# Two residual linear layers with LoRA on one core: where W0's transposition, the small stores and the second weight blocks stand

## The reference

```
x = x + (x W0^T + b0 + (x A0^T) B0)            # base_weight W0, A0, B0 per batch by adapter id
x = x + (x W1^T + b1 + 2 (x A1) B1)            # SCALING = 32/16 = 2
```

## Time and profile before

| | |
|---|---|
| median of 3 runs | 2171.0 us (2167.95 to 2177.97) |
| the profiled execution | 2161.93 us, its span 2160.2 us |
| PE busy | 2076.9 us, 96% of the span |
| DVE busy | 1535.8 us, 71% |
| ACT busy | 738.1 us, 34% |
| POOL busy | 689.3 us, 32% |
| mean DMA rate | 212 GB/s |
| weight matmuls | 3 x 2688 of 128 x 128 x 512 |

### The profile page before, as it was taken

How to read it: one execution, slowest core, us unless ns; L and a number is a source line. 1 busy time by engine, 2 the same in 40 slices (tenths; PEclk the granted TensorE clock), 3 DMA queues, 4 the chain that set the end, 5 groups by cost and what they waited for, 6 DMA issues and landing times.

```text
span 2160.2 us, 27571 instructions
## 1 busy us (share of the span) xinstructions
PE 2076.9 (96%) x9292; PEld 1712.8 (79%) x9292; DVE 1535.8 (71%) x2161; ACT 738.1 (34%) x1294; POOL 689.3 (32%) x498
## 2 busy tenths in 40 slices
PE   6599899999989999999999999999999999999999
PEld 5488687887878788888887888877888788888887
DVE  3367778867778876676876666875767876766875
ACT  5453232323323332333333333332333333333332
POOL 0023121544030445140544130544221445221353
PEclk9799999999999999999999999999999999999999
DMA  9974746798664699474799574789574689574676
GB/s 294 279 239 128 234 145 196 213 277 262 176 185 140 201 266 304 143 222 131 213 259 311 146 224 119 225 246 293 168 217 122 213 242 321 168 215 123 209 218 198
DMA packets 316681, 458.03 MB, mean 212 GB/s; under 512 B 27516, under 2 KB 125820, under 8 KB 316028
## 3 DMA queue, kind: packets, MB, share of 16 engines
q1 hardware_dynamic: 316284, 455.21, 69.9%
q10 hardware_dynamic: 256, 1.05, 0.3%
HBM read 381.70 MB, written 74.45 MB: 211 GB/s over the span
## 4 chain that ended last, share of the span: by engine, by line
PE 73%; DVE 9%; DMA 9%; issue 3%; SPq 2%; ACT 2%; POOL 1%; ACTq 0%; DVEq 0%; POOLq 0%
PE acc L1497 22%; PE acc L1499 21%; PE acc L1498 21%; DMA w_second<-wc_t 4%; DVE w_lo L1031 3%; DMA w_second<-v_t 2%; PE h_acc L1410 2%; PE h_acc L1414 2%; DVE c_out L1193 2%; DVE x_sum L1046 1%; DMA pb_t<-b1d_rows 1%; POOL w_raw L804 1%; DVE c_acc L1132 1%; DVE xop_lo L1056 1%; PE acc L1424 1%
## 5 line engine op out<-in xcount | busy, mean ns | idle before, releaser
L1497 PE MATMUL acc<-xop_hi,w_hi 128*128 128x512 f32 x2688 | 1055.6, 393 | 24.2 <-DVE w_lo L1031 19.1
L804 POOL TENSOR_TENSOR w_raw<-w_raw,w_second 128x512 f32<-128x512 f32 x464 | 652.3, 1407 | 1280.5 <-DMA w_second<-wc_t 862.9
L1498 PE MATMUL acc<-xop_hi,w_lo 128*128 128x512 f32 x2688 | 1048.9, 390 | 0.0
L1499 PE MATMUL acc<-xop_lo,w_hi 128*128 128x512 f32 x2688 | 1048.7, 390 | 0.0
L1031 DVE TENSOR_TENSOR w_lo<-w_raw,w_hi 128x512 fp32r<-128x512 f32 x672 | 568.3, 848 | 446.8 <-ACT w_hi L869 443.7
L869 ACT ACTIVATE w_hi<-w_raw 128x512 fp32r<-128x512 f32 x672 | 423.7, 631 | 1194.7 <-PE acc L1499 980.8
L1497 PEld LDWEIGHTS acc<-xop_hi,w_hi 128*128 128x128 f32 x2688 | 506.2, 188 | 142.1 <-DVE w_lo L1031 31.1
L1499 PEld LDWEIGHTS acc<-xop_lo,w_hi 128*128 128x128 f32 x2688 | 506.1, 188 | 106.4
L1498 PEld LDWEIGHTS acc<-xop_hi,w_lo 128*128 128x128 f32 x2688 | 506.4, 188 | 103.0
L1193 DVE TENSOR_TENSOR c_out<-acc,c_out 128x512 f32<-128x512 f32 x304 | 202.1, 682 | 7.9 <-PE acc L1424 6.2
L1046 DVE TENSOR_TENSOR x_sum<-x_in 128x512 f32<-128x512 f32 x240 | 207.5, 876 | 0.1
(11 more groups left out here) (117 smaller groups left out, 826.7 us busy)
## 6 DMA issues: line engine op xcount, KB each, us to landing
w_raw<-wc_t SPq DMA_DIRECT2D x448, 256.0 KB, 3.8
w_second<-wc_t SPq DMA_DIRECT2D x320, 256.0 KB, 5.0
w_raw<-v_t SPq DMA_DIRECT2D x208, 256.0 KB, 3.8
w_second<-v_t SPq DMA_DIRECT2D x144, 256.0 KB, 5.0
x_in<-x_t SPq DMA_DIRECT2D x128, 256.0 KB, 6.0
out_t<-c_out SPq DMA_DIRECT2D x128, 256.0 KB, 5.4
x_in<-w_t SPq DMA_DIRECT2D x64, 256.0 KB, 5.8
wc_t<-c_out SPq DMA_DIRECT2D x64, 256.0 KB, 5.5
```

The lines of the kernel that those rows point to most:

```text
L804: nc.gpsimd.tensor_tensor(w_raw[:, r, :], w_raw[:, r, :], w_second[:, n % RAW2, :], ALU.add if sign > 0 else ALU.subtract).then_inc(w_summ ...
L1497: nc.tensor.matmul(bank[:, :], wh, xh, start=(k == 0), stop=False)
L1498: nc.tensor.matmul(bank[:, :], wl, xh, start=False, stop=False)
L1499: mm = nc.tensor.matmul(bank[:, :], wh, xl, start=False, stop=end)
```

## The change

- **Transposition of W0.** Units: 4 instead of 8 (a quarter of W0). Parts: 24 instead of 16 (three quarters). Parts are numbered in a list `PARTS`, with the step of M5 at which each is transposed (four still ahead of it) and a list `PART_G_AT` with the step at which its share of G is made: up to two parts in a step, and two G's in M3. G now stands ahead of the step's own matmuls on PE. Four loaded parts are held instead of three.
- **Small stores.** q_rows, qd_rows and b1d_rows are stored at step 2 of M5 instead of in the preamble. b1's rows aren't stored from SBUF: eight DMAs from DRAM to DRAM in M1 bring them to `pb_t`. The loads of b1's rows, of the first parts and of W1's first block stand earlier in the preamble. The load of block (0, 0) of W1 moves to steps 0 and 1 of M3.
- **A1 + A1 W0.** `ag` takes 2 A1 W0 alone, copied by ACT; A1 is loaded again (`a1_row`) and added in passes 2 to 5.
- **U B0 and U b0 spread out.** `p_add` at steps 4, 9, 14, 19 instead of 4, 8, 12, 16; M2's `down` after steps 5 and 7, with the split for M4's at step 12; the second half of `scale_c` in M7 instead of M4; its `turn_c` in M6.
- **Second blocks by ACT's queue.** `load_second`: ACT issues the DMA of `w_second` for step g+5 right behind `w_hi` of step g+2.

The core of the diff:

```diff
+DOWN_AT, A_SPLIT_AT = (1, 3), 8
+DOWN_LATE, A_SPLIT_LATE = (5, 7), 12
...
-    UNITS = [(mg, dg) for dg in (2, 3) for mg in range(GROUPS)]
+    UNITS = [(mg, 2) for mg in range(GROUPS)]
...
-    E_AFTER, Q_AFTER = 3, 5
+    E_AFTER, Q_AFTER = 2, 3
...
-    NPART = 16
-    PIN, PRAW = 3, 4
+    FIRST = [(u // 4, u // 2 % 2 + 2 * (u % 2), at)
+             for u, at in enumerate((-1, -1, -1, -1, 0, 1, 2, 2, 5, 5, 6, 7, 8, 9, 10, 11))]
+    LAST = [(6 + i // 4, i % 4, at) for i, at in enumerate((3, 3, 4, 4, 12, 13, 14, 15))]
+    PARTS = sorted(FIRST + LAST, key=lambda p: p[2])
+    PIN, PRAW = 4, 4
+    PART_G_AT = [1, 1, 2, 2, 3, 3, 4, 4, 5, 5, 6, 6, 7, 7, 8, 9, 10, 11, 12, 13, 14, 15, 16, 17]
...
-        P_ADD_AT = (4, 8, 12, 16)
+        P_ADD_AT = (4, 9, 14, 19)
+        C_TURN_AT = ((M7, 2), (M6, 6))
...
@@ SP, load_w @@
-                for oh, dh in second:
...
-                    sp.dma_start(w_second[:, n % RAW2, :], w_t[oh * MH + m, :, col:col + SW]
-                                 ).then_inc(wb_loaded[n % RAW2], 16)
@@ SP, load_a @@
+                sp.dma_start(a1_row[:, :, :], lora_a1[bass.ds(adapter_of(1, b), 1), :, :]
+                             .rearrange("o p (k r) -> (o p) k r", r=RANK)).then_inc(a1_row_loaded, 16)
@@ SP, preamble @@
-                if t == 1:
                     for b in range(BATCH):
                         sp.dma_start(b1_rows[b * RANK:(b + 1) * RANK, :],
...
-                if t == 4:
+                if t == 1:
                     sp.wait_ge(a1_lo_ready, 1)
                     sp.wait_ge(t_filled, B_USE + 4)
+                    for n in range(PIN):
+                        load_part(n)
                     for k in range(KH):
                         load_x(0, 1, 1, k)
...
-                    sp.dma_start(q_t[:, :], q_rows[:, :]).then_inc(small_stored, 16)
-                    sp.dma_start(qd_t[:, :], qd_rows[:, :]).then_inc(small_stored, 16)
-                    for i, rows in enumerate((b1_rows[:, 0:DIM // 2], b1_rows[:, DIM // 2:], b1d_rows[:, :])):
-                        sp.dma_start(pb_t[i, :, RANK:R2, :], rows).then_inc(small_stored, 16)
@@ SP, loop over g @@
                 if g == 2:
+                    sp.dma_start(q_t[:, :], q_rows[:, :]).then_inc(small_stored, 16)
+                    sp.dma_start(qd_t[:, :], qd_rows[:, :]).then_inc(small_stored, 16)
+                    sp.dma_start(pb_t[2, :, RANK:R2, :], b1d_rows[:, :]).then_inc(small_stored, 16)
+                if q == M1 and j < BATCH:
+                    sp.dma_start(pb_t[0:2, j, RANK:R2, :].rearrange("h r n -> r h n"),
+                                 lora_b1[bass.ds(adapter_of(1, j), 1), :, :].rearrange("o r (h n) -> (o r) h n", h=2)
+                                 ).then_inc(b1_stored, 16)
...
-                if g == NPART - 4:
+                if q == M3 and j < 2:
                     sp.wait_ge(part_filled, 2 * NPART)
-                if NPART - 4 <= g < NPART - 2:
-                    for k in range(4 * (g - NPART + 4), 4 * (g - NPART + 4) + 4):
+                    for k in range(4 * j, 4 * j + 4):
                         load_x(0, 0, 0, k)
@@ POOL @@
-                    pool.wait_ge(small_stored, 5 * 16)
                     pool.wait_ge(b1d_ready, 1)
@@ ACT @@
+            def load_second(s):
+                if not (STEPS <= s < NG and is_sum_w(s)):
+                    return
...
+                if n >= RAW2:
+                    act_e.wait_ge(w_summed, STEPS + n - RAW2 + 1)
+                else:
+                    act_e.wait_ge(g_turned, GROUPS)
+                col = (dh * KH + h * KS) * P
+                act_e.dma_start(w_second[:, n % RAW2, :], w_source(pl)[oh * MH + m, :, col:col + SW]
+                                ).then_inc(wb_loaded[n % RAW2], 16)
...
+            act_e.wait_ge(h_bias_stored, 16)
...
                 if g + 2 < NG:
                     w_split_hi(g + 2)
+                load_second(g + 2 + RAW2)
@@ DVE @@
                 if t == Q_AFTER:
                     dve.wait_ge(t_copied, Q_USE + 4)
+                    dve.wait_ge(v_stored[0], NU // 2 * 16)
...
-                if q == M3 and 3 <= j < 3 + GROUPS:
-                    add_to_ag(j - 3)
...
-                if pl < PRE and i in (M3, M4):
+                if pl < PRE and i in (M3, M7):
                     scale_c(pl * 2 * KT + (0 if i == M3 else KT) + j)
@@ PE @@
+                    for n in range(NPART):
+                        if PART_G_AT[n] == s:
+                            add_part_g(n)
+                    turns = [(n, mm) for n in PARTS_AT.get(s, []) for mm in range(2)]
...
-                    if q == 0:
-                        add_part_g(s)
...
-                    if i in DOWN and j in (1, 3):
-                        down(q, range(0, KS) if j == 1 else range(KS, KH))
+                    down_at = DOWN_LATE if is_late(pl, i) else DOWN_AT
+                    if i in DOWN and j in down_at:
+                        down(q, range(0, KS) if j == down_at[0] else range(KS, KH))
```

More of the change, by code:

```diff
@@ L182, in two_layer_lora_kernel, with ended, sum_parts @@
     Q_USE = unit_use(Q_AFTER, 3) + 1
-    T_USES = unit_use(NU - 1, 3) + 1
-    NPART = 16
-    PIN, PRAW = 3, 4
-    def part(u):
-        return u // 4, u // 2 % 2, u % 2
+    T_USES = Q_USE + 4
+    FIRST = [(u // 4, u // 2 % 2 + 2 * (u % 2), at)
+             for u, at in enumerate((-1, -1, -1, -1, 0, 1, 2, 2, 5, 5, 6, 7, 8, 9, 10, 11))]
+    LAST = [(6 + i // 4, i % 4, at) for i, at in enumerate((3, 3, 4, 4, 12, 13, 14, 15))]
+    PARTS = sorted(FIRST + LAST, key=lambda p: p[2])
+    NPART = len(PARTS)
+    PART_OF = {p[:2]: n for n, p in enumerate(PARTS)}
+    PARTS_AT = {g: [n for n, p in enumerate(PARTS) if p[2] == g] for g in range(-1, STEPS)}
+    PIN, PRAW = 4, 4
+    PART_G_AT = [1, 1, 2, 2, 3, 3, 4, 4, 5, 5, 6, 6, 7, 7, 8, 9, 10, 11, 12, 13, 14, 15, 16, 17]
+    PART_ENDS = {max(n for n, p in enumerate(PARTS) if p[0] == pair): pair for pair, _, _ in PARTS}
+    def ended(n):
+        return sum(e < n for e in PART_ENDS)
+    def sum_parts(s):
+        pair, h = s // 4, s // 2 % 2
+        return PART_OF[pair, h], PART_OF[pair, h + 2]
     def x_bank(ns):
@@ L287, in two_layer_lora_kernel @@
         ag = over("ag", [P, BATCH, KT, RANK], fp32, "c_out", 32 * K1)
-        ag_k = over("ag_k", [P, KT, BATCH, RANK], fp32, "c_out", 40 * K1)
+        a1_row = over("a1_row", [P, KT, RANK], fp32, "q_half")
         acc = [pb(f"acc{i}") for i in range(BANKS)]
@@ L964, in _ @@
                 x_split_hi(0, k)
-            copy_g(3)
             w_split_hi(1)
-            for u in range(2, 4):
+            for n in range(2, 4):
                 for mm in range(2):
-                    copy_part(u, mm)
-            split_part_hi(0)
+                    copy_part(n, mm)
             for g in range(NG):
@@ L1259, in _ @@
                     w_split_lo(g + 2)
-                if g + 1 < NPART:
-                    split_part_lo(g + 1)
+                for n in range(NPART):
+                    if PART_G_AT[n] == g + 1:
+                        split_part_lo(n)
                 if j == 4 and i in (M4, M3) and PRE <= pl < NPL:
```

300 lines of the change are left out of this document (154 added, 146 removed).

## The result

The changed kernel takes 2148.0 us in the median of 4 runs (2142.3 to 2151.5), the kernel before beside it 2169.6 (2168.0 to 2178.0): a ratio of 0.9907 (95%: 0.9884 to 0.993), 21.6 us less. The forecast was 2127, 44 us less. The sign was right, the size twice too large.

What follows compares the result with a forecast made beforehand. The prediction took TensorE, busy 96% of the span, as the bound, with gains left only before 839.3 us. Terms for preamble, M5, M3, M2, M1, M7/M6 and second blocks summed to -44, from 2171.0 to 2127 us; range 2105 to 2149.

Steps and rivals of the forecast that it cites:

- Preamble, -41 forecast: Before the first product: the wait for the b1d_rows store goes and work moves out, so M5 starts at 67.0, not 107.8.
- I take nothing: those loads start at 36, and by 46.5 most have landed: Preamble: nothing added for a late second store of v, issued near 46.5; at worst M5 would start at 73.
- rival B: M5: DMA bounds it, as stretches of mostly writes recur; +12 us, 2139 in all; chance 14%.
- M5, +15 forecast: First product, M5: more transposed parts and G's on PE make it 102.3 us long instead of 87.4.
- M2, -6.5 forecast: M2, first pass: most of the 8.4 us stall before the down product goes; -5.5 in the second pass.
- One store and reload now has 5 steps, where it had 4: M2: the 9.5 us store and reload of q_half gets 13.9 us between p_adds, the ground for -6.5.
- M1, M7, M6: Half of scale_c leaves M4 for M7: M1 -4.5 and -3.5 by pass, M7 and M6 +2.5 per pass.
- M6 has 23.0 of 44.4 and takes the rest: M6: DVE, busy 23.0 of 44.4 us, absorbs what overflows M7's 48.9; bounds 0 and 6 per pass.
- Second blocks, -4 forecast: Late passes: loading second blocks by ACT's own queue saves 4 us; bounds -9 and +10.
- A: Rival: DVE relief frees M2 and M1 wholly, M7 costs nothing, late passes lose nothing; 2112 us; chance 16%.
- C: Rival, late passes: second blocks landing in over 6.3 us lengthen every three steps; at 7.0, 2235 us; chance 4%.
- D: Rival, preamble: the wait only moves, b1d_rows or bias store landing near 90, M5 at 100; 2160 us; chance 3%.

Runs made afterwards that it cites:

- e6: Changed kernel with bias stored as rows, SP's preamble order altered, p_add every 6 steps with M2's down product later, second half of scale_c in M4: 2125.6 us, ratio 0.9809.
- e11: e6 with the eight loads of x block (1, 0) at steps 3 to 6 of M3 instead of 8 to 11: 2122.4 us, ratio 0.9785.
- e1: Changed kernel with SP's preamble order altered: second store of v before the x loads, bias store between the fourth and fifth: 2145.8 us, ratio 0.9883.
- e5: Changed kernel with the bias stored in rows of 520 bytes instead of 128 packets of 4 bytes: 2140.3 us, ratio 0.988.
- e9: Kernel before with only the bias store changed, to rows of 520 bytes: 2160.6 us, ratio 0.9945.
- e12: Changed kernel with the stores of q, qd and b1d back ahead of the part stores, POOL waiting for them: 2163.4 us, ratio 0.9955.
- e2: Changed kernel with p_add every 6 steps instead of every 5 and M2's down product at steps 8 and 10: 2140.9 us, ratio 0.9856.
- e14: e11 with the loads and split of A from the third pass on in M4 instead of M6: 2124.6 us, ratio 0.9796.
- e3: Changed kernel with the second half of scale_c back in M4 instead of M7, in both passes: 2139.7 us, ratio 0.9856.
- e10: Kernel before with one part of the change alone, second blocks loaded by ACT's queue: 2163.3 us, ratio 0.9963.
- e4: Changed kernel with the second blocks loaded by SP's queue again: 2162.4 us, ratio 0.9967.
- e7: Changed kernel with the loads and split of A from the third pass on back in M4: 2146.3 us, ratio 0.9912.

## Why the prediction was partly wrong, point by point

**Preamble, -41 forecast, -32.3 measured.** The mechanism was right: the old wait went, and the row of work that remains ends at 67 to 68 when no transfer disturbs it (67.6 in e6, 66.9 in e11; forecast 67.0). The step that failed is "I take nothing: those loads start at 36, and by 46.5 most have landed". SP issued the store of v at 52.07, since I had not added up SP's time for the x loads ahead of it (11.2 us), and it landed at 64.9 behind a hole of 6 to 7 us, which the bias store tears. Each alone is enough to be late: with the order mended the x loads lie in the hole (e1, 73.3), and without the hole M5 still starts at 69.9 (e5). The hole was in the rows I read (80 to 100: share 0.99 at 159 GB/s), and I put it down to writes in general (rival B). It was the store of 128 values of 4 bytes (e5: 5.6 us, e9: 7.2 us of M5's start). The worst case that I wrote down, 73, was still 2.5 too small.

**M5, +15 forecast, +17.5 measured.** The count of transposes and G's holds; PE is busy 101.5 of 104.9 us. Rival B did not come true: the small stores cost nothing there (e12).

**M2, -6.5 forecast, -0.7 measured.** The step "One store and reload now has 5 steps, where it had 4" failed: M2 still stands 8.6 us over M4. In the changed kernel the wait for q_half of the earlier trace rows is still there, but behind it stand late weight blocks: with 6 steps the wait is gone and M2 is as long, 57.6 (e2). Some 4 to 5 us of it are transfers (e11, e14), since the x block that the change moved into M3 adds 2 MB to a stretch in which the next x block, the A1 + A1 W0 store and M2's first blocks are loaded (e11). That the edits don't interact was assumed, not read. In pass 1, where no x block was moved, M2 did fall (-4.0 of -5.5), so the step may have been right for the kernel before; no run tests it there.

**M1, M7, M6.** M1 gained 2.6 and 2.1 (-4.5 and -3.5 forecast). With `scale_c` back in M4 it is only 1.0 longer (e3), not much more than its scatter from trace to trace: the relief that the forecast counted on was hardly there. M4, where `scale_c` stood, has 49.0 us with and without it. M7 and M6 lost 7.6 and 3.2 instead of 2.5 each, and e3 takes back 5.6 and 3.7 of it. The step that failed is "M6 has 23.0 of 44.4 and takes the rest", with w_lo "some 4 us ahead of PE". DVE's busy time in M7 was forecast too high, if anything (48.9; it was 46.6 of 46.9 us): a step of `scale_c` took 1142 ns and not 842, but those of `w_lo` there 748 instead of 937. The backlog wasn't hidden, though. M6 alone lost 5.2 and 3.1 us, in pass 0 two of the `scale_c` ran in it, and PE waited for `w_lo` in M7 and M6 of pass 0 (us, times, longest), where before it waited 0.3 us in all:

```profile
PEld acc L1551 <- DVE w_lo L1073: 7.6, 6, 3.2
```

**Second blocks, -4 forecast, +0.9 between the two profiled executions.** This row doesn't refute the term. The kernel before's late passes took 1320.9 us in its profiled execution and 1331.6 in e9's, with the same code, while the means of all traces with one queue and with two are 1330 and 1320. As a part by itself it is worth 8 us of the whole (e10, medians) and 14 in the changed kernel (e4), so -4 was rather too small. Most of the 7 us by which the medians differ more than the profiled executions may lie here; that is an inference from the table above, since the runs that make up the medians have no traces. The move of the A loads from M4 to M6, which the prediction didn't price, costs nothing measurable with the second queue there (e7, e14). Of the two rules of the Trainium skill that the prediction set against each other ("DMA: Bandwidth & Descriptors", on rings and on issuing engines), the runs refute neither: the term isn't 0, and the chain no longer waits for second blocks, but they do not show whether that comes by overtaking in the queues or by the time that SP's sequencer saves.

**Rivals and range.** A's premise (DVE freed, M7 free of cost) is wrong, C and D did not occur: the second blocks land in 4.4 us, well under the 6.3 from which C decides. The 2148.0 lies inside the range, but by its slow end and by luck: that end was made of 12 us for M5, which didn't come, and not of what was lost in the preamble, M2 and M6. The fast end of 2105 doesn't follow from the bounds given with it; they lead to 2117.

The best version, e11, runs at 0.9785 of before, 47 us less. It keeps the transposition in M5, the small stores' new place and the second queue, undoes the move of `scale_c`, and adds four edits: the bias as rows, SP's order in the preamble, p_adds every 6 steps with M2's down product later, and the earlier loads of x block (1, 0).
